# Dealing the next batch's context steps earlier: 2, 2, 2, 2 behind the band tiles, one fewer behind the norm, the first cross query and the last MLP matmuls

## What is computed

```python
x = x + attn(layernorm(x))             # 16 heads of 16, relative positions clipped at +-20
x = x + xattn(layernorm(x), ctx, ctx)  # ctx: 1601 tokens x 256, 16 heads of 64
x = x + ffn(layernorm(x))              # gated, 704 wide, blockwise FP4 on both operands
```

```python
Kn = layernorm(ctx) * g + b                      # also the values' input
k, v = split(Kn @ wk), split(Kn @ wv)
out = (l2norm(q) @ l2norm(k).T) @ v              # no softmax
x = Q + out @ wo + bo
return x + gelu(layernorm2(x) @ w1 + b1) @ w2 + b2
```

## Time and profile before

| | |
|---|---|
| median of 3 runs | 3123.89 us (3121.35 to 3126.41) |
| the profiled execution's own time | 3123.3 us |
| its span, first to last instruction | 3121.5 us, so 1.8 us lie around it |
| mean granted TensorE clock | 0.946 of full |
| busy: PE / DVE / POOL / ACT | 86% / 57% / 42% / 39% |

### The profile page before, as it was taken

How to read it: one execution, slowest core, us unless ns; L and a number is a source line. 1 busy time by engine, 2 the same in 40 slices (tenths; PEclk the granted TensorE clock), 3 DMA queues, 4 the chain that set the end, 5 groups by cost and what they waited for, 6 DMA issues and landing times.

```text
span 3121.5 us, 51792 instructions
## 1 busy us (share of the span) xinstructions
PE 2691.9 (86%) x15346; PEld 1844.6 (59%) x15346; DVE 1772.3 (57%) x4053; ACT 1219.7 (39%) x2184; POOL 1295.8 (42%) x1038
## 2 busy tenths in 40 slices
PE   3687899788997899878997899978998889978998
PEld 2465566555665656555665556656575656655565
DVE  5746545666456654665456564656546664565636
ACT  1237223453235423362234532364234622354323
POOL 2543344424434244433444254343444344342544
PEclk8899899989999899998999999999999989998999
DMA  8518001860048300780028500582007800394006
GB/s 241 123 33 196 29 0 49 179 157 1 7 99 194 86 1 7 166 188 25 1 57 184 144 1 7 114 195 69 1 15 168 202 1 1 78 193 114 1 7 135
DMA packets 487136, 270.72 MB, mean 87 GB/s; under 512 B 218619, under 2 KB 482644, under 8 KB 483540
## 3 DMA queue, kind: packets, MB, share of 16 engines
q1 hardware_dynamic: 449636, 260.78, 34.6%
q10 hardware_dynamic: 37152, 5.90, 1.9%
HBM read 136.11 MB, written 130.50 MB: 85 GB/s over the span
## 4 chain that ended last, share of the span: by engine, by line
PE 63%; DMA 10%; DVE 8%; issue 8%; SPq 5%; ACT 4%; POOL 2%; ACTq 0%; DVEq 0%; POOLq 0%
PE PS L1574 58%; DMA prob_scr<-arena 9%; PE PS L1577 5%; SPq L599 1%; ACT arena L1084 1%; DVE arena L479 1%; SPq L587 1%; ACT arena L1091 1%; SPq L578 1%; POOL rstd L429 1%; SPq L682 1%; DVE arena L1284 0%; DVE qrc L453 0%; DVE arena L477 0%; DVE cbn L1251 0%
## 5 line engine op out<-in xcount | busy, mean ns | idle before, releaser
L1574 PE MATMUL PS<-arena 128*17 128x128 f32 (+6 forms) x6864 | 806.7, 316 | 141.7 <-ACT arena L1084 127.6
L1574 PEld LDWEIGHTS PS<-arena 128*17 128x17 f32 (+3 forms) x6864 | 542.1, 127 | 347.3 <-ACT arena L1084 164.1
L1577 PE MATMUL PS<-ident,arena 128*128 128x128 f32 x3362 | 541.8, 290 | 106.3 <-DVE arena L1277 39.7
L1577 PEld LDWEIGHTS PS<-ident,arena 128*128 128x128 f32 x3362 | 406.7, 148 | 295.4 <-issue 143.6
L1356 DVE CUSTOM_DVE_ANT_0 PS<-PS,arena 128x512 f32<-128x512 f32 x512 | 346.4, 707 | 230.5 <-DMA arena<-bias_scr 138.1
L1574 PE MATMUL PS<-cwk,arena 128*128 128x512 f32 (+1 forms) x936 | 470.5, 627 | 2.7 <-ACT arena L977 2.7
L429 POOL TENSOR_TENSOR crn<-crn,mhalf 128x8 f32<-128x8 f32 (+1 forms) x234 | 419.3, 1798 | 123.8 <-DVE crn L1265 122.1
L1084 ACT ACTIVATE arena<-PS,nmax 128x512 f32<-128x512 f32 x512 | 344.3, 700 | 205.6 <-DMA prob_scr<-arena 145.3
L972 ACT ACTIVATE arena<-PS 128x512 f32<-128x512 f32 (+1 forms) x234 | 139.6, 597 | 683.5 <-PE PS L1574 683.5
L869 POOL TENSOR_TENSOR arena<-arena,mass_mask 128x512 f32<-128x512 f32 x128 | 163.8, 1280 | 410.1 <-ACT arena L1084 391.1
L1574 PEld LDWEIGHTS PS<-cwk,arena 128*128 128x128 f32 (+1 forms) x936 | 181.6, 199 | 147.1 <-issue 133.1
(11 more groups left out here) (161 smaller groups left out, 3684.6 us busy)
## 6 DMA issues: line engine op xcount, KB each, us to landing
arena<-bias_scr SPq DMA_DIRECT2D x130, 336.0 KB, 4.4
prob_scr<-arena SPq DMA_DIRECT2D x128, 336.0 KB, 4.9
bias_scr<-arena SPq DMA_DIRECT2D x132, 256.0 KB, 5.4
q_scr<-arena SPq DMA_DIRECT2D x144, 128.0 KB
arena<-q_scr SPq DMA_DIRECT2D x132, 128.0 KB, 5.5
arena<-k_scr SPq DMA_DIRECT2D x18, 768.0 KB, 12.1
arena<-prob_scr SPq DMA_DIRECT2D x128, 80.0 KB, 4.1
arena<-far_scr SPq DMA_DIRECT2D x18, 546.0 KB, 7.5
```

Of the source, the lines that this page charges most:

```text
L1574: return pe.matmul(o, l, r, start=start, stop=stop, **kw)
L1577: return pe.transpose(o, i, ident[0:i.shape[0], 0:i.shape[0]])
```

## The change

The dictionary `SLOTS_AT` alone changes; no instruction is added, removed or altered in form.

```diff
-SLOTS_AT = {("band", 0): (-6, -5), ("band", 1): (-4,), ("band", 2): (-3,), ("band", 3): (-2,),
-            ("wo", 0): (-1,), ("wo", 1): (0,), ("wo", 2): (1,), ("wo", 3): (2,), "ln": (3, 4, 5, 6),
-            ("x", -1): (7, 8, 9), ("x", 0): (10, 11, 12), ("x", 1): (13, 14), ("x", 2): (15, 16), ("x", 3): (17, 18),
-            "yn": (19, 20, 21), ("h", 1): (22,), ("h", 3): (23,), ("h", 5): (24,), ("h", 7): (25,)}
+SLOTS_AT = {("band", 0): (-6, -5), ("band", 1): (-4, -3), ("band", 2): (-2, -1), ("band", 3): (0, 1),
+            ("wo", 0): (2,), ("wo", 1): (3,), ("wo", 2): (4,), ("wo", 3): (5,), "ln": (6, 7, 8),
+            ("x", -1): (9, 10), ("x", 0): (11, 12, 13), ("x", 1): (14, 15), ("x", 2): (16, 17), ("x", 3): (18, 19),
+            "yn": (20, 21, 22), ("h", 1): (23,), ("h", 3): (24,), ("h", 5): (25,), ("h", 7): ()}
```

## The result

| | before | after |
|---|---|---|
| median, same chip | 3122.62 us | 3150.61 us (3147.3 to 3153.38) |
| the profiled execution's own time | 3123.3 us | 3147.3 us |
| its span | 3121.5 us | 3145.5 us |

A forecast was written before the change was run, and what follows sets the result against it. PE was taken to bound the kernel, through its idle time and its time at 1.2 GHz. Terms summed to +1.05 us a batch, +8.4 us for eight; forecast 3131.5 us, range 3108 to 3150 us.

The forecast's parts named there:

- band tiles, idle time and lone transposes: Bands 1 to 3: PE's waits and transposes that stand alone add 2.15 us a batch.
- band tiles, clock: Band stretch: 12.3 us at half clock a batch, which gives -1.6 us; bounds -7.75 and +2.5 us.
- output projections: Second output projection: slot 2's products cover the 1.31 us wait for ACT's L1131, -1.3 us a batch.
- norm: Norm stage: PE's 3.4 us stop behind DVE's L1277 stays with one slot fewer behind it, 0 us.
- first cross query, wait: First cross query with two slots: PE waits 2.4 us behind DVE's L1464 where it waited 0.1, +2.3 us a batch.
- clock behind it: Behind the first cross query's new wait: half clock may follow, between 0 and +1.75 us; +0.9 taken.
- slot 13: Slot 13, now last of tile 0: a 2.1 us wait replaces 2.7 us and 1.75 us of clock is saved, -2.35 us.
- last Gelu: Behind the last MLP pair: nothing covers the last Gelu any more, so PE stands, +0.95 us a batch.
- band 1: Slots -4 and -3: waits of 0.5, 0.8 and 1.8 us replace one of 1.24 us, +1.9 us a batch.
- Band 2: Slots -2 and -1: the 1.91 us wait stays; +0.65 us between the two steps, +0.2 for lone transposes.
- the second fall should last about half as long: Behind band 2's wait: more key projections and products follow, shortening half clock; 12.3 us in the band tiles overall.
- rival 2: Both new waits, at the cross queries, drop the clock: 3.65 us a batch slower, 3152.5 us; chance 0.17.

The follow-up runs named there:

- the two kernels with the old band tiles on one chip: Slot from behind MLP matmul 5 moved to the end of tile 0, against the kernel before: 0.9943; the kernel before with zero matmuls in its band tiles: 0.984.
- the repetition: The changed kernel again, unaltered, on one of the slower chips, against the kernel before: 1.011.
- 8 of 8 with the old band tiles: The changed kernel with band tiles 2, 1, 1, 1 again and their three slots back in the norm; against the kernel before 1.0065.
- the query part alone: The kernel before with only the first cross query's third slot moved into the norm: 1.0047.
- the MLP part: The kernel before with only the MLP's last slot moved into the norm, making slot 13 the last of tile 0: 0.9981.
- the band part alone: The kernel before with only the band tiles changed to 2, 2, 2, 2 slots, paid for by three of the norm's four: 1.002.
- with the band tiles filled: The kernel before with zero-valued matmuls added in its band tiles, against the kernel before: 0.984.

## Why the prediction was right in its sign and wrong in its size

| term, us a batch | forecast | measured |
|---|---|---|
| band tiles, idle time and lone transposes | +2.15 | +1.6 in the waits, +0.6 in busy time |
| band tiles, clock | -1.6 | 0 |
| output projections | -1.3 | -1.6 |
| norm | 0 | +0.7 |
| first cross query, wait | +2.3 | +2.8 |
| clock behind it | +0.9 | +1.2 |
| slot 13 | -2.35 | -2.5 |
| last Gelu | +0.95 | +0.86 |
| rest of that stage, the attention with it | 0 | -0.9, of which -0.7 is clock |
| sum | +1.05 | +2.8 |

**What bounds the kernel** held: no other engine came near a bound, and the differences are PE's waits, its clock and 0.6 us of its own work in the band tiles.

**The sum fell short by the clock.** In the forecast the terms of the clock were -1.6 in the band tiles, +0.9 at the query and -1.75 at slot 13, -2.45 us a batch, and the waits +3.5. Measured, the clock gave nothing over a batch (34.3 us at half clock before, 34.1 after), so that the waits and the work stood alone, +2.8. That the forecast had the right sign is in part luck: it is the small difference of the two, and the larger error was in the clock.

**The waits** held nearly all. The 1.31 us at the second output projection, the 3.4 us in the norm, slot 13's 2.1 us (1.84) and the last Gelu's 0.95 us (0.86) came where they were put, and slot 13 gave its 2.5 us, which two other kernels show again. In band 1 the forecast was too high, +1.9 us for +1.2 to +1.5: of its 0.5, 0.8 and 1.8 us the middle one is 0.47 us in five batches and missing in three. Band 2 made up for it, 0.7 to 0.9 us between its two steps for 0.65.

**The step that failed first** is "the second fall should last about half as long", 12.3 us at half clock in the band tiles. They kept 16.64 us, the mean of before; that the two agree to the hundredth is chance, as single batches lie between 13.7 and 27.3 us. The reason given, that more key projections and products follow each wait, doesn't decide it: filling the same places with the same zero matmuls brought 1.5 to 1.7% with the denser slots and 1.6% without. Around each 1.9 us wait PE's work stayed sparse (`weigh_band`, lone transposes, another wait of 0.5 to 0.9 us), as the slots -4 to -1 that came there have no products; that this is the reason was not tested. On this point the Trainium skill, "TensorE: Matmul & The Clock Gate", section "HAM oscillation - how this bites in real kernels", advises to put the matmuls together so that the engine stays at its higher clock; the change does so in part, and the trace shows no gain from it. The same section of the Trainium skill counts half of the time at the lower clock as lost. The runs agree with that roughly: between the two kernels with the old band tiles on one chip, without and with zero matmuls, there are 12.4 us fewer at half clock in the band stretch, an estimate of 6.2 us by that section of the Trainium skill, and the stretch got 5.8 us shorter, with the zero matmuls' own time inside.

**The norm** was put at nothing. Its wait did stay, but the clock behind it did not: 5.12 us at half clock a batch instead of 2.99, in this batch 6.8 us from 1119.0. The prediction priced the clock in the band tiles, at the first cross query and at slot 13, and took it as fixed at all other places.

**The first cross query.** The mechanism was right, a chain of DVE and POOL laid bare, and its size was short by 0.4 us, 2.4 for 2.79: the forecast let L1464 start 0.7 us after L1284, and it started 1.18 us after. Whether the clock falls behind it was the open question; it does in 5 of 8 batches here, 2 of 8 in the repetition, 8 of 8 with the old band tiles. As a mean of runs the half price, 0.9 us, was fair. It is the term that decides the case: returning that slot alone brings the time back to that of the kernel before.

**The range.** 3150.6 us is almost what rival 2 gave, 3152.5, but not by its mechanism: that had slot 13's new wait of 1.84 us drop the clock too, and it does in no batch of any kernel that has it. A number that fits is not yet a mechanism that does. What the range left out is that the band's and the norm's clock could both go the wrong way at once.

**What stays open.** The three parts tried alone are together the whole change, the norm's slots included. They sum to +0.48% (0.20, 0.47 and -0.19), the whole to 0.9 or 1.1%. The traces show two effects that only the whole has or that the parts count twice: the longer L1284 (0.74 us more wait a batch, 0.2%), and the falls that the query part alone saves at slot 13, where the whole and the MLP part save them anyway (5/8 of 1.7 us a batch, 0.3%). Together they are as large as the gap, but no run isolates them. Why the clock falls behind one wait in some batches and not in others was not settled. It is not free at each place, though: in 16 batches of the changed kernel, from its two traces, half clock in the norm lasts 3.4 us in six, and in all six the clock falls behind the query's wait; it lasts 6.8 us in ten, and in only one of these does it fall there. So the measured +0.7 in the norm and +1.2 at the query belong together: in 15 of the 16 batches 3.4 us at half clock, beside the norm's own 3.4, lie either at the one place or at the other.

## What to carry to other kernels

Before a piece of cover is moved to where it seems more useful, add up the chain on other engines that it covers at its old place, here 2.9 us of POOL's root and two operations of DVE: the slot there was worth 2.8 us a batch, and no other move of the change was worth as much. Price a change of TensorE's clock wait by wait, with a part of its own for every wait that stays, and test it by filling the waits with zero-valued matmuls: this costs a few lines, tells clock from idle time, and here it was itself worth more than any reordering (0.984, and 0.975 with slot 13 moved). Effects of single moves need not add up where the clock has a share in them, so undoing one part of the whole says more than doing one part alone.

## What the runs showed of the hardware

- The same wait does not always drop the clock. Behind the 2.67 us at slot 13 it falls in 8 of 8 batches in the kernel before, 0 of 8 with the band part alone, 3 of 8 with the query part alone, 7 of 8 with the band tiles filled; behind the 2.79 us at the first cross query in 5 and in 2 of 8 batches of the changed kernel in its two traces, and in 8 of 8 with the old band tiles. What lies ahead of the wait differs between these kernels, and for some the chip; the 5 and the 2 are one program on two chips.
- Zero-valued bf16 matmuls keep the granted clock up. Four of eight batches of the kernel before have their band tiles at 1.00 throughout with them (24.6 us in the one shown), where the earlier trace rows have 0.65 and 0.70; the other four still have 3.4 to 13.7 us at half clock there.
- L1284, a 128x512 product on DVE, took 1.25 us instead of 0.69 in every kernel whose first cross query held slots 9 and 10, and 0.69 with slots 8 and 9. In the changed kernel these are 8 of its 234 executions, and all others take 0.68 or 0.69. In both kernels POOL works on a root beside it, so this alone is not the cause; it was not found.
